# Paged attention on one core: the rotated heads turned by transposing DMAs instead of TensorE, with rows laid out position by batch

## The chip, the cores and the metric

The kernel runs on one core of a Trainium2 chip. The metric is the device time of one execution in microseconds; lower is better. Names of engines: TensorE (PE in the profile, PEld for its weight loads), VectorE (DVE), ScalarE (ACT), GpSimd (POOL), and SyncE (SP), which here only issues DMAs.

## The reference

`x` is 64 sequences of 32 positions by 512. Two residual layers follow each other; the second is where this change lies.

```python
x = x + L0(x)                                   # 512x512 product, weights quantized to a codebook plus LoRA
q = (x @ Wq.T).reshape(64, 32, 32, 128)         # 32 query heads
k = (x @ Wk.T).reshape(64, 32, 8, 128)          # 8 key heads
v = (x @ Wv.T).reshape(64, 32, 8, 128)
q, k = rope(rmsnorm(q, q_norm_w), pos), rope(rmsnorm(k, k_norm_w), pos)
k_all = concat([k_cache[block_table], k])       # 16 pages of 32 keys, then the 32 new ones
v_all = concat([v_cache[block_table], v])
probs = softmax(mask(q @ k_all.T / sqrt(128)))  # 4 query heads share a key head
x = x + (probs @ v_all).reshape(64, 32, 4096) @ Wo.T
```

## The kernel before

**Tiles and units.** 128 rows, 4 sequences of 32 positions, make a tile; there are 16 tiles, and each is done twice, once per half of the heads (4 key heads and 16 query heads), so the tile loop runs over 32 tiles. A tile has 16 units: 4 sequences ("batches") times 4 key heads. A unit's 128 query rows are 4 query heads of one key head by 32 positions of one batch. Most products are made of 16-bit high and low parts, three matmuls for one product.

**What a unit does.** `tile_block` writes every engine's program by hand, slot by slot (one slot per unit). On TensorE: scores of unit s against 512 cached keys (line 1204) and the 32 new ones (1207), the transposes of the probabilities of unit s-2 (1215), the output against the values of unit s-3 (1238, 1240), the turn of its new-key columns (1220). VectorE takes the row maxima (1448), normalises (1459) and makes low parts (1453, 1466); ScalarE does the exponentials (1353) and high parts. Scores of a unit wait until the maxima of the one before have been read from the single bank `Sp`.

**Heads of the next tile.** Between these, a tile also projects the next tile's heads, group by group: keys (group 0), queries (1, 3, 4, 5) and values (2). The table `TILE_PLAN` says in which slot each step stands: `proj` on TensorE, `squares` and `scale` on ScalarE, `root` and `add` on GpSimd, `rope` on VectorE. GpSimd's `add` ends the rotation: `qr` then holds 128 rows by 4 heads of 128 in 32 bits. Before the change `turn_rotated` transposes the four heads on TensorE into the bank `TRp` (line 1270, slots 5, 6, 10, 12, 14), and `rotated_high` on ScalarE (1397) and `rotated_low` on VectorE (1493) write high and low parts of it to `qT` or `kTn`, putting the columns batch by batch on the way. A tile's first scores wait for the last `tr_lo` of the tile before. `TRp` also serves 40 of the 56 weight pieces that are split during the loop (line 1281).

**SyncE's queue.** SyncE works through one list per batch: page numbers into registers, a wait for the maxima of the batch three back, that batch's mask (line 696), weight pieces where due (713, 716), the sixteen page loads of 64 KB for a buffer that has come free (688), and then, by the batch's place in the tile, stores and loads of new values (699, 703), the rope table (709), `xT` (706), the residual rows (1109, 1113). There are three page buffers, so pages are loaded two batches ahead. In the first 15 tiles or so the weight pieces add loads and stores to this list.

**Values.** GpSimd gathers the value rows of the next batch, four indirect DMAs per batch, in the slots set by `((0, 1), (2,), (3,), ())`.

**Before the loop.** A set-up block prepares caches and weights; at its end SyncE loads the first four tiles of `x` (line 447) and the first weights (449), and all engines meet at a barrier. `first_block` then makes the first layer's result for 16 tiles and the first tile's heads; its SyncE list loads `x` (776), stores the result (778) and its turned rows (781), loads weights (395) and the first pages.

## Time and profile before

| | us |
|---|---|
| runs, median of 3 (2249.0 to 2250.43) | 2250.25 |
| the profiled execution, whole time | 2244.9 |
| its span in the profile | 2243.0 |
| TensorE busy in the span | 2158.3 |
| first scores of the tile loop at | 306.30 |

The span runs from the first to the last instruction of the profiled execution; its whole time lies 1.9 us above it, and the median of the runs 5.35 us above that. Times in rows count from the span's start. A row of a timeline gives start, length, engine, line, operation and tiles; where TensorE's rows overlap, one matmul's end is still in the array while the next begins, so starts are compared with starts. A row of the SyncE queue is the time its issue took, not the transfer.

### The profile page before, as it was taken

How to read it: one execution, taken by the hardware profiler on the slowest of the kernel's cores; microseconds unless marked ns; L12 is line 12 of the kernel's file. 1: busy time of each engine (PE TensorE's matmuls, PEld its weight loads, DVE VectorE, ACT ScalarE, POOL GpSimd, SP SyncE). 2: the span in 40 equal slices, each digit the busy share in tenths (PEclk: the TensorE clock that was granted, in tenths of full speed). 3: DMA queues.
4: the chain of work that ended last, by engine and by line, in shares of the span. 5: the costliest groups of instructions: out<-in, count | busy, mean ns of one | idle time of the engine just before them, and what ended most of it. 6: DMA issues, size and time to landing. Idle time of an engine off the chain costs nothing.

```text
span 2243.0 us, 61281 instructions
## 1 busy us (share of the span) xinstructions
PE 2158.3 (96%) x18068; PEld 1411.6 (63%) x18068; DVE 1727.7 (77%) x3942; ACT 1465.5 (65%) x4967; POOL 1251.3 (56%) x2067
## 2 busy tenths in 40 slices
PE   5786989999999999999999999999999999999998
PEld 2343556666666666666666666666666666666665
DVE  6995668777777777777777777777777777777785
ACT  2542557676677776676676667667666666666664
POOL 3422126656666655665656666666656566665663
PEclk9997999999999999999999999999999999999999
DMA  3687658667667667667669667666566656666663
GB/s 103 221 279 248 222 167 238 195 193 207 200 194 207 197 191 216 203 198 211 198 191 300 179 189 238 185 177 175 175 188 181 181 173 186 183 178 177 184 178 104
DMA packets 478727, 438.06 MB, mean 195 GB/s; under 512 B 53037, under 2 KB 407676, under 8 KB 477886
## 3 DMA queue, kind: packets, MB, share of 16 engines
q1 hardware_dynamic: 433278, 295.70, 44.7%
q0 software_dynamic: 40960, 134.25, 19.6%
q10 hardware_dynamic: 4160, 4.19, 0.5%
q8 instruction: 149, 2.44, 0.4%
q14 instruction: 180, 1.47, 0.2%
HBM read 377.24 MB, written 56.70 MB: 193 GB/s over the span
## 4 chain that ended last, share of the span: by engine, by line
PE 84%; DVE 1%; issue 0%; ACT 0%; DVEq 0%; ACTq 0%
PE PR L1257 21%; PE Op L1238 15%; PE WOp L1296 15%; PE Sp L1204 15%; PE PTp L1215 11%; PE TRp L1270 3%; PE Sp L1207 1%; PE Op L1220 1%; PE Op L1240 1%; PE TRp L1281 1%; DVE masked L1448 0%; PE WOp L1281 0%; ACT masked L1353 0%; DVE WoT L1507 0%; DVE OT L1466 0%
## 5 line engine op out<-in xcount | busy, mean ns | idle before, releaser
L669 POOL DMA_INDIRECT pages<-values_split,rows x512 | 526.4, 1028 | 104.0 <-issue 78.5
L1347 ACT ACTIVATE pts<-PTp 128x512 f16<-128x512 f32 x512 | 305.7, 597 | 363.9 <-PE PTp L1215 363.8
L1257 PE MATMUL PR<-Wt,xT 128*128 128x512 f16 x2232 | 539.1, 380 | 0.0
L1238 PEld LDWEIGHTS Op<-pts,pages 128*128 128x128 f16 x6144 | 385.4, 98 | 121.1 <-DVE OT L1466 4.2
L1238 PE MATMUL Op<-pts,pages 128*128 128x128 f16 x6144 | 426.6, 219 | 2.4 <-DVE OT L1466 2.3
L1204 PE MATMUL Sp<-pages,qT 128*128 128x512 f16 x1536 | 416.2, 380 | 6.9 <-PEq L184 6.9
L1448 DVE CUSTOM_DVE_ANT_0 masked<-Sp,mask 128x544 f32<-128x544 f32 x512 | 370.0, 723 | 60.4 <-PE Sp L1207 54.3
L1453 DVE TENSOR_TENSOR pts<-PTp,pts 128x512 f16<-128x512 f32 x512 | 351.5, 686 | 75.1 <-ACT pts L1347 74.9
L1353 ACT ACTIVATE masked<-masked,small 128x544 f32<-128x544 f32 x512 | 379.0, 740 | 9.4 <-DVE small L1448 8.5
L1296 PE MATMUL WOp<-WoT,OT 128*128 128x512 f16 x1536 | 377.5, 379 | 0.0
L1466 DVE TENSOR_TENSOR OT<-Op,OT 128x128 f16<-128x128 f32 x512 | 148.2, 289 | 266.3 <-ACT p L1341 262.7
L1257 PEld LDWEIGHTS PR<-Wt,xT 128*128 128x128 f16 x2232 | 218.6, 98 | 187.6 <-issue 1.7
L1215 PE MATMUL PTp<-ident,masked 128*128 128x128 f32 x2048 | 325.1, 281 | 0.6 <-DVE pts L1453 0.6
L1558 POOL CAST n<-masked 128x64 f16<-128x64 f32 x512 | 120.8, 236 | 354.0 <-DVE masked L1459 217.6
L1459 DVE TENSOR_SCALAR masked<-masked,small 128x544 f32<-128x544 f32 x512 | 280.7, 548 | 18.2
L1362 ACT ACTIVATE OT<-Op 128x128 f16<-128x128 f32 x512 | 145.6, 284 | 205.3 <-PE Op L1220 197.0
L1296 PEld LDWEIGHTS WOp<-WoT,OT 128*128 128x128 f16 x1536 | 145.0, 98 | 116.4
L1215 PEld LDWEIGHTS PTp<-ident,masked 128*128 128x128 f32 x2048 | 214.2, 140 | 1.0 <-issue 0.8
L1204 PEld LDWEIGHTS Sp<-pages,qT 128*128 128x128 f16 x1536 | 142.3, 98 | 96.9 <-issue 8.2
L1551 POOL TENSOR_TENSOR qr<-qr,rs_ 128x512 f32<-128x512 f32 x155 | 196.8, 1270 | 0.0
L1207 PEld LDWEIGHTS Sp<-kTn,qT 128*128 128x128 f16 x1536 | 113.7, 97 | 121.4 <-issue 1.0
L1546 POOL TENSOR_TENSOR small<-small 128x4 f32<-128x4 f32 x155 | 181.9, 1174 | 12.9
(211 smaller groups left out, 3075.5 us busy)
## 6 DMA issues: line engine op xcount, KB each, us to landing
pages<-keys_transposed SPq DMA_DIRECT2D x2048, 64.0 KB
mask<-mask_rows SPq DMA_DIRECT2D x128, 128.0 KB
v<-new_values SPq DMA_DIRECT2D x96, 128.0 KB
weights_split<-wdst SPq DMA_DIRECT2D x40, 256.0 KB
keys_transposed<-pages SPq DMA_DIRECT2D x32, 256.0 KB, 3.4
values_split<-pages SPq DMA_DIRECT2D x16, 512.0 KB, 3.6
rope_s<-rope_table SPq DMA_DIRECT2D x32, 256.0 KB
pages<-values_split,rows POOLq DMA_INDIRECT x512
```

Source lines behind the costliest of these rows:

```text
L669: nc.gpsimd.indirect_dma_start(out=vS[:, n % 2, c, :, :].rearrange("p l n -> p (l n)"), out_offset=None, in_=v_d, in_offset=bass.IndirectO ...
L1204: nc.tensor.matmul(Sp[:, 512:1024].rearrange("p (a n) -> p a n", a=NPP), qT[:, tt, ql, q0:q0 + P], kT[n % KBUFS][:, :, h, kl, :], start=(k ...
L1215: m = nc.tensor.transpose(PTp[:, c * P:(c + 1) * P], masked[:, u % 3, S + c * P:S + (c + 1) * P], ident[:, :])
L1238: nc.tensor.matmul(o, vS[:, par, c, low, h * D:(h + 1) * D], pts[:, u % 2, part, c * P:(c + 1) * P], start=(k == 0), stop=False)
L1257: m = nc.tensor.matmul(bank(k), xT[:, c, xl, :], Wp[:, c, wl, GROUP_COL[k]:GROUP_COL[k] + HID], start=(i == 0), stop=(i == NPASS - 1))
L1296: m = nc.tensor.matmul(WOp[:, :], OT[:, 1 - tt, hq, ol, :], WoT[:, hq, wl, :], start=(hq == 0 and ol == 0 and wl == 0), stop=(hq == QHH - ...
L1347: nc.scalar.activation(pts[:, u % 2, 0, :], PTp[:, :], ACT.Copy).then_inc(G.pt_hi, 1)
L1353: nc.scalar.activation(masked[:, u % 3, :], masked[:, u % 3, :], ACT.Exp, bias=nmax[u % 2], scale=-1.0, accum_out=psum_row[u % 2]).then_in ...
L1448: V.tensor_tensor_reduce(out=masked[:, u % 3, :], in0=Sp[:, 512 - S:1024], in1=mask[:, par, :], scale=-SCALE, scalar=BIG, op0=ALU.add, op1 ...
L1453: V.tensor_tensor(pts[:, u % 2, 1, :], PTp[:, :], pts[:, u % 2, 0, :], ALU.subtract).then_inc(G.pt_lo, 1)
L1459: V.tensor_scalar(masked[:, u % 3, :], masked[:, u % 3, :], rinv[u % 2], None, ALU.mult).then_inc(G.norm_done, 1)
L1551: nc.gpsimd.tensor_tensor(qr[:, m_ % 2, :], qr[:, m_ % 2, :], rs_[:, :], ALU.add).then_inc(G.rope_done, 1)
```

## The change

The rotated heads are no longer transposed by TensorE. ScalarE and VectorE split `qr` into 16-bit high and low parts in a new tile `split` (two buffers), and SyncE issues one transposing DMA per group, 128 rows by 1024 columns, from `split` into `qT` or `kTn`. The first tile's heads, in `first_block`, are still turned by TensorE.

- `turn` in the plan now names places in SyncE's list: the batch in the tile, and which third of the page loads the DMA stands before (3: after them). `split` names the slots of the two halves of the split.
- [...] The scores read a batch's columns with a step of four elements (`b::BPT`), in `qT` and `kTn` alike.
- `qr` has one buffer instead of two; three small tables move into other memory.
- A tile's scores wait per key head, at the first batch, for the DMA of that head (`heads_turned`), instead of for all of `tr_lo`.
- Of the output product's early parts (`wo`), three matmuls move from slot 8 to slot 7 and three from slot 7 to slot 5.
- The fourth value gather of a batch is issued one slot earlier.

```diff
-    turn={5: 0, 6: 1, 10: 3, 12: 4, 14: 5}, turned={6: 0, 7: 1, 11: 3, 13: 4, 15: 5},
-    wo={4: (0, 1), 7: (1, 2), 8: (2, 3), 9: (3, 4), ...
+    split={5: 0, 7: 1, 10: 3, 12: 4, 14: 5}, turn={(0, 3): 0, (1, 1): 1, (2, 0): 3, (2, 3): 4, (3, 0): 5},
+    wo={4: (0, 1), 5: (1, 2), 7: (2, 3), 9: (3, 4), ...
...
                 for t in range(4):
-                    sp.dma_start(xin[:, t, :], x_d[t]).then_inc(G.x_first, 16)
+                    for b in range(BPT):
+                        sp.dma_start(xin[b::BPT, t, :], x_d[t, b * S:(b + 1) * S, :]).then_inc(G.x_first, 16)
...
         def load_table(sp, tile):
-            sp.dma_start(rope_s[:, :], rope_d[tile % TILES]).then_inc(G.table_loaded, 16)
+            for b in range(BPT):
+                sp.dma_start(rope_s[b::BPT, :], rope_d[tile % TILES, b * S:(b + 1) * S, :]).then_inc(G.table_loaded, 16)
...
                         if t < TPS + 4:
-                            sp.dma_start(out_d[t - 4], x1b[t % 2]).then_inc(x1_stored[t % 2], 16)
+                            for b in range(BPT):
+                                sp.dma_start(out_d[t - 4, b * S:(b + 1) * S, :], x1b[t % 2][b::BPT, :]).then_inc(x1_stored[t % 2], 16)
...
+                    def turn_heads(ti, k):
+                        m_ = norm_no(ti, k)
+                        sp.wait_ge(G.split_low, m_ + 1)
+                        sp.dma_start(turned_heads((ti + 1) % 2, k), split[:, m_ % 2, :, :].rearrange("p l n -> p (l n)"), transpose=True).then_inc(heads_turned[NORMED.index(k)], 16)
...
-                            for part in (range(0, 5), range(5, 10), range(10, NPP)):
+                            for third, part in enumerate((range(0, 5), range(5, 10), range(10, NPP))):
+                                if past >= 0 and ti in proj and (b, third) in plan["turn"]:
+                                    turn_heads(ti, plan["turn"][b, third])
                                 load_pages(sp, numbers, batch % KBUFS, part)
...
+                        if ti in proj and (b, 3) in plan["turn"]:
+                            turn_heads(ti, plan["turn"][b, 3])
...
-                        if u % UPT == 0 and u > 0:
-                            pe.wait_ge(G.tr_lo, len(NORMED) * (u // UPT))
-                        q0 = (h * BPT + b) * P
+                        if b == 0 and u >= UPT:
+                            if h == 0:
+                                pe.wait_ge(heads_turned[0], 16 * (u // UPT))
+                            pe.wait_ge(heads_turned[h + 1], 16 * (u // UPT))
+                        q = [qT[:, tt, h, part, b::BPT] for part in range(2)]
...
-                    def rotated_high(ti, tt, k):
-                        a.wait_ge(G.tr_done, norm_no(ti, k) + 1)
-                        src, dst = rotated(tt, k, 0)
-                        nc.scalar.activation(dst, src, ACT.Copy).then_inc(G.tr_hi, 1)
+                    def rotated_high(ti, k):
+                        m_ = norm_no(ti, k)
+                        a.wait_ge(G.rope_done, m_ + 1)
+                        if m_ >= 2:
+                            before, kb = divmod(m_ - 2, len(NORMED))
+                            a.wait_ge(heads_turned[kb], 16 * (before + 1))
+                        nc.scalar.activation(split[:, m_ % 2, 0, :], qr[:, :], ACT.Copy).then_inc(G.split_high, 1)
...
                         if m_ >= 1:
-                            v.wait_ge(G.rope_done, m_)
+                            v.wait_ge(G.split_low, m_)
...
-                    def rotated_low(ti, tt, k):
-                        v.wait_ge(G.tr_hi, norm_no(ti, k) + 1)
-                        src, dst = rotated(tt, k, 1)
-                        _, high = rotated(tt, k, 0)
-                        V.tensor_tensor(dst, src, high, ALU.subtract).then_inc(G.tr_lo, 1)
+                    def rotated_low(ti, k):
+                        m_ = norm_no(ti, k)
+                        v.wait_ge(G.split_high, m_ + 1)
+                        V.tensor_tensor(split[:, m_ % 2, 1, :], qr[:, :], split[:, m_ % 2, 0, :], ALU.subtract).then_inc(G.split_low, 1)
...
-                            for c in ((0, 1), (2,), (3,), ())[place]:
+                            for c in ((0, 1), (2, 3), (), ())[place]:
                                 gather(m + 1, c)
```

How the instructions move, at the places that matter. TensorE, from the end of slot 6 to the scores of slot 7 of a tile, before:

```order
L1238 MATMUL Op<-pts,pages 128x128 x12
L1240 MATMUL Op<-p,v 128x128
L1220 MATMUL Op<-ident,n 128x128
L1270 MATMUL TRp<-ident,qr 128x128 x4
L1204 MATMUL Sp<-pages,qT 128x512 x3
L1207 MATMUL Sp<-kTn,qT 128x32 x3
```

and with the change, at the same place:

```order
L1245 MATMUL Op<-pts,pages 128x128 x12
L1247 MATMUL Op<-p,v 128x128
L1227 MATMUL Op<-ident,n 128x128
L1211 MATMUL Sp<-pages,qT 128x512 x3
L1214 MATMUL Sp<-kTn,qT 128x32 x3
```

The four transposes into `TRp` are gone, at this place and at the four others of each tile.

VectorE, slots 5 and 6 of a tile with the change (line 1483 is the low part of the split, 1477 and 1478 are the rotation, 1487 the new values):

```order
L1441 ISA masked,small<-Sp,mask 128x544
L1441 ISA small 128x1
L1483 TENSOR_TENSOR split<-qr,split 128x512
L1446 TENSOR_TENSOR pts<-PTp,pts 128x512
L1477 TENSOR_TENSOR qr<-qn,rope_s 128x512
L1478 TENSOR_TENSOR rs_<-qn,rope_s 128x512
L1450 RECIPROCAL small<-small 128x1
L1452 TENSOR_SCALAR masked<-masked,small 128x544
L1459 TENSOR_TENSOR OT<-Op,OT 128x4x32
L1441 ISA masked,small<-Sp,mask 128x544
L1441 ISA small 128x1
L1487 SCALAR_TENSOR_TENSOR vn<-PR,vn 128x512
```

Before, the key heads' low part stood one slot later, just ahead of the new values; now it stands in the slot of the rotation of the first query group, after that slot's maxima.

SyncE, at the turn of a tile's last two batches, with the change (line 689 is a page load and the register step before it):

```order
L689 ISA
L689 DMA pages<-keys_transposed 128x256
L1113 DMA_TRANSPOSE qT<-split 128x8x128
L704 DMA v<-new_values 32x2048 x3
L684 DMA page_no<-page_numbers 1x128
L675 TENSOR_LOAD page_no
L697 DMA mask<-mask_rows 128x512
L1113 DMA_TRANSPOSE qT<-split 128x8x128
L689 ISA
L689 DMA pages<-keys_transposed 128x256
```

Before, the same list had no row between the last page load and the new values, nor between the mask and the next page loads.

## Rows read from the trace of the kernel before

**Rows 1.** The page's busy time of each engine, with its share of the span.
```profile
PE 2158.3 (96%) x18068; PEld 1411.6 (63%) x18068; DVE 1727.7 (77%) x3942; ACT 1465.5 (65%) x4967; POOL 1251.3 (56%) x2067
```

**Rows 2.** The page's chain that ended last: shares by engine and by line.
```profile
PE 84%; DVE 1%; issue 0%; ACT 0%; DVEq 0%; ACTq 0%
PE PR L1257 21%; PE Op L1238 15%; PE WOp L1296 15%; PE Sp L1204 15%; PE PTp L1215 11%; PE TRp L1270 3%; PE Sp L1207 1%; PE Op L1220 1%; PE Op L1240 1%; PE TRp L1281 1%; DVE masked L1448 0%; PE WOp L1281 0%; ACT masked L1353 0%; DVE WoT L1507 0%; DVE OT L1466 0%
```

**Rows 3.** Timeline of TensorE, 1240 to 1249 us: start, length, line, tiles.
```profile
1247.23 0.61 PE L1270 MATMUL TRp<-ident,qr 128*128 128x128 f32 x4
1247.67 0.81 PE L1204 MATMUL Sp<-pages,qT 128*128 128x512 f16 x3
1248.32 0.23 PE L1207 MATMUL Sp<-kTn,qT 128*128 128x32 f16 x3
1248.40 0.63 PE L1215 MATMUL PTp<-ident,masked 128*128 128x128 f32 x4
```

**Rows 4.** Timeline of the SyncE queue, one batch from 1235 us.
```profile
1235.05 0.32 SPq L696 DMA_DIRECT2D mask<-mask_rows  x1
1235.55 9.05 SPq L688 DMA_DIRECT2D pages<-keys_transposed  x16
```

**Rows 5.** SyncE's own waits: 366 to 1204, 1384 to 2102, 305 to 366 us.
```profile
SPq L696 <- DVE small L1448: 137.1, 53, 5.4
...
SPq L696 <- DVE small L1448: 158.3, 49, 4.6
...
SPq L713 <- PE WOp L1281: 5.1, 6, 1.8
```

**Rows 6.** Timeline of the SyncE queue: the load of xT in two early and two late tiles.
```profile
412.46 0.58 SPq L706 DMA_DIRECT2D xT<-x_transposed  x1
...
473.56 0.58 SPq L706 DMA_DIRECT2D xT<-x_transposed  x1
...
1803.25 0.43 SPq L706 DMA_DIRECT2D xT<-x_transposed  x1
...
1863.03 0.43 SPq L706 DMA_DIRECT2D xT<-x_transposed  x1
```

**Rows 7.** DMA view: a queue's share; issues by tile, size, us to landing.
```profile
q1 hardware_dynamic: 433278, 295.70, 44.7%
...
new_values<-vn SPq DMA_DIRECT2D x32, 256.0 KB, 2.3
...
pages<-in_L_cond_Wv SPq DMA_DIRECT2D x1, 1024.0 KB, 8.6
```

**Rows 8.** Timeline of the SyncE queue, 193 to 222 us.
```profile
194.07 1.79 SPq L447 DMA_DIRECT2D OT<-in_x  x4
195.91 0.43 SPq L449 DMA_DIRECT2D pages<-in_L_cond_Wk  x1
204.80 0.25 SPq L764 DMA_DIRECT2D page_no<-page_numbers  x1
...
205.52 0.50 SPq L709 DMA_DIRECT2D rope_s<-rope_table  x1
...
221.07 0.95 SPq L395 DMA_DIRECT2D pages<-in_L_cond_Wv  x1
```

**Rows 9.** Timeline of the first block: TensorE at 231 us, SyncE's queue at its end.
```profile
231.39 0.60 PE L849 MATMUL Op<-ident,pages 128*128 128x128 f32 x4
...
301.89 0.43 SPq L781 DMA_DIRECT2D x_transposed<-pts  x1
```

**Rows 10.** Groups by line and shape: weight loads of 16-bit and of 32-bit rows.
```profile
L1215 PEld LDWEIGHTS PTp<-ident,masked 128*128 128x128 f32 x2048 | 214.2, 140 | 1.0 <-issue 0.8
...
L1207 PEld LDWEIGHTS Sp<-kTn,qT 128*128 128x128 f16 x1536 | 113.7, 97 | 121.4 <-issue 1.0
```

**Rows 11.** Timeline of GpSimd and of ScalarE at unit 5 of a tile.
```profile
1238.96 1.27 POOL L1551 TENSOR_TENSOR qr<-qr,rs_ 128x512 f32<-128x512 f32 x1
...
1240.53 0.31 ACT L1341 ACTIVATE p<-Op 128x128 f16<-128x128 f32 x1
```

More of the change, by code:

```diff
@@ L129, in build @@
         qn = sb("qn", [P, 2, HID], F32)
[L130 removed]
+        qr = sb("qr", [P, HID], F32)
+        split = sb("split", [P, 2, 2, HID], F16)
         rs_ = sb("rs_", [P, HID], F32)
@@ L702, in load_new_values @@
             for place, part in enumerate((0, 1, 0)):
-                sp.dma_start(v5[place * S:(place + 1) * S, tile % 2, :, :], vn_d[tile % 2, part].rearrange("(b p) n -> p b n", b=BPT)).then_inc(v5_loaded[tile % 2], 16)
+                sp.dma_start(v5[place * S:(place + 1) * S, tile % 2, :, :], vn_d[tile % 2, part].rearrange("(p b) n -> p b n", b=BPT)).then_inc(v5_loaded[tile % 2], 16)
         def load_xT(sp, tile):
@@ L1079, in pieces_before @@
                 return sum(g < slot for g in piece_at)
-            def turns_before(slot):
-                return sum(UPT * t + sl < slot for t in proj for sl in plan["turn"])
             def unit(u):
@@ L1316, in _ @@
                             output(ti, tt, *plan["wo"][sl])
-                        if ti in proj and sl in plan["turn"]:
-                            turn_rotated(ti, plan["turn"][sl], sl)
                         if s in piece_at:
@@ L1410, in _ @@
                             new_probs(s - 3)
-                        if ti in proj and sl in plan["turned"]:
-                            rotated_high(ti, tt, plan["turned"][sl])
+                        if ti in proj and sl in plan["split"]:
+                            rotated_high(ti, plan["split"][sl])
                         if s - 1 in piece_at:
@@ L1516, in _ @@
                         if ti in proj:
-                            if sl in plan["turned"]:
-                                rotated_low(ti, tt, plan["turned"][sl])
+                            if sl in plan["split"]:
+                                rotated_low(ti, plan["split"][sl])
                             if sl == plan["values_low"]:
```

85 lines of the change are left out of this document (32 added, 53 removed).

## The prediction

> **What bounds the kernel now.** I read four views in turn. The busy shares first: TensorE is at 96%, the next engine, VectorE, at 77% [rows 1]. The chain that ended last says the same in another way: 84% of the span is TensorE, and the turning of rotated heads (line 1270) alone is 3% of the chain [rows 2]. Then TensorE's timeline inside a tile: the transposes of one head group begin at 1247.23 us and the next unit's scores at 1247.67 us, back to back with no idle time before either [rows 3]. So in the tile loop whatever leaves TensorE's stream shortens the kernel, as long as nobody else becomes late. Last, the SyncE queue, because that is where the work goes: for each batch of four units it issues sixteen page loads in about 9.05 us [rows 4], and the only wait it has left in the loop is for the maxima of the batch before (line 696). That wait is its slack: 137.1 us from 366 to 1204 us and 158.3 us from 1384 to 2102 us [rows 5]. From one load of xT to the next a tile takes 473.56 - 412.46 = 61.1 us in the first stretch and 59.8 us in the second [rows 6]; that is 13.7 and 12.0 tiles, so SyncE has 10.0 us to spare per early tile and 13.2 us per late one.
>
> **What leaves TensorE.** In the tile loop 155 turns (31 tiles, five each, four transposes a turn) are removed. A turn takes 1247.67 - 1247.23 = 0.44 us of the stream [rows 3]; 3% of 2243 us over 155 gives 0.43 us [rows 2]. Gain: 155 x 0.435 = 67.5 us, or 2.2 us a tile. The five turns of the first block stay.
>
> **What the other engines do instead.** ScalarE's and VectorE's halves of the split have the same size, 128 x 512, as the two evacuations they replace, now from SBUF and mostly a slot earlier. Do they find their input? For the key heads ScalarE gets to the place at 1240.53 + 0.31 = 1240.84 us, and GpSimd's addition has ended at 1238.96 + 1.27 = 1240.23 us [rows 11]: 0.6 us in hand, so no wait. The second order fence shows the piece on VectorE: rotation and split now fall in one slot. It is the same work per tile in a tile 2.2 us shorter; I allow 0.1 us a tile of lateness, 4 us in all. The earlier value gathers cost nothing: GpSimd issues the same four per batch, behind the new columns TensorE waits for.
>
> **What SyncE takes over.** Per tile, five transposing DMAs of 256 KB, and four rope loads instead of one. A single load takes the queue 0.43 to 0.50 us [rows 6, 8]; three smaller ones more make 1.25 us. A transposing DMA occurs nowhere in this trace. Below, it cannot cost less than a plain issue, 0.43 us [rows 8]; above, if the queue were held from issue until the data has landed, it would cost what a 256 KB store of similar size takes to land, 2.3 us [rows 7]. I take 1.4 us, the middle: neither row is near, since the queue has more to describe than for a copy but has no need to wait for the landing. With a price T per DMA a tile asks 1.25 + 5T of SyncE and gives back 2.2 us less time:
> early tiles gain the smaller of 2.2 and 10.0 - 1.25 - 5T; at T = 1.4 that is 1.75, a shortfall of 0.45 us x 14 tiles = 6 us. Late tiles gain the smaller of 2.2 and 13.2 - 1.25 - 5T = 4.95: all of it, in 16 tiles.
> The first tile has no such slack. There SyncE waits only 5.1 us, for weight pieces [rows 5], and 1.25 + 7 = 8.25 us are added: 3 us late. Bytes are no worry: 155 x 256 KB = 40.6 MB beside the 295.70 MB that took 44.7% of the DMA engines [rows 7], about 6 points more at the same rate.
> Behind a turn that waits for its split stand page loads and masks, two batches ahead of their use; the last turn of a tile is issued at the tile's end and needed by its fourth unit, three units of some 3.7 us later.
>
> **Before the loop.** The rows of inputs now go position by batch, so each 128-row load or store of x becomes four of 32 rows.
> The first x loads: 4 issues took 1.79 us, from 194.07 us on, the stage load behind them went at 195.91 us, and everything stood until 204.80 us [rows 8]. Twelve more issues at 1.79 / 4 = 0.45 us push that load back by 5.4 us, and nothing else runs there: 5 us, directly on the path.
> First block: the value weights were issued at 221.07 us [rows 8], take 8.6 us to land [rows 7], so about 229.7 us, and TensorE turns them at 231.39 us [rows 9]. Ahead of them come 1.25 us of rope loads and two steps with six more DMAs, less a gap: some 5.3 us later, so 235.0 us, 3.6 us too late.
> Its end: in the last four steps, up to the last store of the turned rows at 301.89 us [rows 9], SyncE is nearly always issuing, pages among the stores; four steps with three more stores are 5.2 us, and some 1.7 us of gaps absorb part: 3.5 us.
>
> **Strided reads.** The stationary rows of the scores now step over four elements (8 bytes), and no load of weights in this trace does that. Where 512 columns follow, a load is hidden behind them; the three loads for the new keys are not, since their matmuls come 0.08 / 3 = 0.027 us apart [rows 3]. Upper bound: a weight load of twice the bytes takes 140 ns and not 97 [rows 10], 43 ns x 1536 = 66 us, the whole gain. Lower bound: 0; a gain is excluded, since the same columns are read. I take 0: the strided load uses as many bytes as before, and the row of as many bytes is the one of 97 ns.
> The Trainium skill (SBUF — State Buffer, "Specifications (TRN2)") asks for two hits per 16-byte line for full bandwidth, and 8-byte steps give just two: by it the cost would be 0 as well, against the 66 us of the row. No run here shows it yet.
>
> **Sum.** -67.5 + 6 + 3 + 4 + 5 + 3.6 + 3.5 = -42.4 us. The profiled execution took 2244.9 us (span 2243.0 us), the median of the runs 2250.25 us, 5.35 us above; so 2202.5 us against the profile and **2208 us** against the median. Own range of this case: T = 1.2 with the smaller losses left out (up to -61 us) gives 2189; T = 1.7 (early tiles gain 0.25 us, the first loses 2.45) gives -3.5 - 35.2 + 2.45 + 16.1 = -20 us, 2230.
>
> **Rivals.**
> *SyncE becomes the bound (slower).* Place: the turns among the page loads; price: T. Early tiles lose once T passes 1.75, late ones keep the full 2.2 up to T = 1.95. The late tiles' -16 x 2.2, the early ones' 14 x (5T - 8.75), the first tile's 1.25 + 5T - 5.1 - 2.2 and the 16.1 us of the four other losses come to zero at T = 1.97: above that the kernel is slower. If the eight 128 x 128 blocks of a DMA are each issued like one small transfer (8 x 0.32 us [rows 4], T = 2.56), early tiles lose 4.05 us each, late ones 0.85, the first 6.75: 57 + 14 + 7 + 16 = 94 us, so 2344 us; at T = 2.3 it is 2303 us. For it: all is issued by one queue, in order, that is busy 84% of an early tile. Against: single issues of up to 1 MB took under 1 us [rows 8]. Chance 0.24.
> The Trainium skill speaks for it: VectorE: DVE Perf Modes, "The three transpose paths", gives 1309 ns for a 128 x 128 transpose by DMA against 390 ns on TensorE. If eight such followed one another with the queue held, T would be an estimated 10.5 us and the kernel beyond 3500 us; no run here shows it, and I give that extreme 0.03 of the 0.24.
> *Strided weight loads are slow.* The three short matmuls per unit wait; up to 66 us back: 2208 to 2274 us. For: nothing hides them. Against: they are 1536 short loads of the same bytes. Chance 0.09.
> *VectorE is late.* Split and rotation in one slot leave the probabilities' low halves late, TensorE waits in two or three slots per tile, 0.5 to 1 us a tile: 2223 to 2239 us. Chance 0.07.
> That the change does less than it says (turns still on TensorE) is excluded by the first order fence.
>
> **How the numbers follow.** Forecast 0.60 (2189 to 2230). Within 0.2% (4.5 us, about what a measurement can tell) lie T near 1.95 and a strided cost near its middle. Faster: 0.60 + 0.07 + 0.03 of strided reads = 0.70; same 0.06; slower 0.24. The range 2188 to 2290 holds the forecast, VectorE late, strided reads and the mild part of the SyncE rival; it leaves out T above 2.2, about 0.15.
>
> **What would show it.** Right: line 1270 gone, a late tile near 57.6 us, SyncE still waiting for maxima a few us per late tile, single DMA_TRANSPOSE rows near 1.4 us, the tile loop beginning some 12 us later. Wrong: SyncE without waits in the loop and TensorE idle before the scores of a tile's first units, released by a DMA; or the short score matmuls further apart than 0.027 us.

## The result, and the profile after

The changed kernel takes 2422.3 us (median of 4 runs, 2404.8 to 2431.4) against 2249.6 us (4 runs): a ratio of 1.076, 95% interval 1.070 to 1.083. It is 172.7 us **slower**; the forecast was 2208 us and the range ended at 2290 us. The profiled execution of the changed kernel took 2418.0 us, its span 2416.1 us.

The page of the changed kernel: busy time by engine, the load of SyncE's transfers (q1), and the chain that ended last.

```profile
PE 2169.8 (90%) x17448; PEld 1405.8 (58%) x17448; DVE 1725.4 (71%) x3942; ACT 1472.2 (61%) x4967; POOL 1263.9 (52%) x2067
...
q1 hardware_dynamic: 590814, 336.36, 55.0%
...
PE 45%; SPq 22%; issue 7%; DMA 6%; DVE 4%; ACT 2%; another core or an unknown queue 1%; DVEq 0%; ACTq 0%; POOL 0%
SPq L689 14%; PE WOp L1288 10%; PE PR L1264 9%; PE Op L1245 9%; PE Sp L1211 8%; PE PTp L1222 6%; DMA rope_s<-rope_table 4%; SPq L1113 3%; SPq L711 2%; DMA qT<-split 1%; PE Sp L1214 1%; SPq L704 1%; DVE qr L1477 1%; SPq L675 1%; DVE rs_ L1478 1%
```

Before, 84% of the chain was TensorE [rows 2]; now 45% is, and SyncE's queue with its transfers holds 28%. Among the links stands one that the prediction hardly spoke of: the load of the rope table. TensorE has 620 transposes less to do and yet a larger busy time than before [rows 1]; a lower granted clock will explain that.

The waits of VectorE, of TensorE and of the SyncE queue over the changed kernel's span (us in total, times, longest):

```profile
DVE qr L1477 <- DMA rope_s<-rope_table: 142.6, 30, 6.6
```
```profile
PE Op L1245 <- DVE OT L1459: 117.5, 49, 5.6
...
PE Sp L1211 <- DMA qT<-split: 12.9, 6, 5.0
```
```profile
SPq L697 <- DVE small L1441: 119.6, 55, 4.6
```

In every tile but the first the rotation of the key heads waits 142.6 / 30 = 4.75 us for the table; before, it waited once, 0.6 us. TensorE's long wait is for VectorE. SyncE still waits for maxima, 119.6 us in all, but, as will be seen, not in the batch where it would count. How one stall runs its course is in the chain of waits of the changed kernel, 1725 to 1739 us (start, length, what):

```profile
1725.26 4.15 DMA rope_s<-rope_table
1729.43 0.69 DVE qr L1477
1730.12 0.60 DVE rs_ L1478
...
1731.25 0.30 DVE OT L1459
1731.60 0.84 PE Op L1245 x12
...
1732.61 1.28 PE WOp L1288 x3
1733.89 1.28 PE Sp L1211 x3
...
1738.13 0.65 PE WOp L1288 x3
```

The four table loads of line 711 stand at the end of SyncE's list for a tile, behind the last turn and 16 page loads. The last one lands 4.15 us after the start of its issue. The rotation (lines 1477, 1478) runs then, and behind it, in VectorE's order, stands the low half of the output product (line 1459), for which TensorE's next value products wait.

Why the table is issued so late shows where the list of a tile's last batch is set beside the rotation that needs the table. The kernel before, SyncE's queue and VectorE:

```profile
1632.69 1.32 SPq L703 DMA_DIRECT2D v<-new_values  x3
...
1638.80 0.34 SPq L696 DMA_DIRECT2D mask<-mask_rows  x1
...
1648.01 0.42 SPq L709 DMA_DIRECT2D rope_s<-rope_table  x1
```
```profile
1654.15 0.68 DVE L1486 TENSOR_TENSOR qr<-qn,rope_s 128x512 f32<-128x512 f32 x1
```

and the changed kernel:

```profile
1708.30 1.27 SPq L1113 DMA_TRANSPOSE qT<-split  x1
1709.67 1.43 SPq L704 DMA_DIRECT2D v<-new_values  x3
1712.17 0.35 SPq L697 DMA_DIRECT2D mask<-mask_rows  x1
1712.63 1.25 SPq L1113 DMA_TRANSPOSE qT<-split  x1
1714.07 9.34 SPq L689 DMA_DIRECT2D pages<-keys_transposed  x16
1723.46 2.39 SPq L711 DMA_DIRECT2D rope_s<-rope_table  x4
```
```profile
1729.43 0.69 DVE L1477 TENSOR_TENSOR qr<-qn,rope_s 128x512 f32<-128x512 f32 x1 [4.42 <-DMA rope_s<-rope_table]
```

Before, the mask, which heads the list, starts 15.35 us ahead of the rotation, after a wait for maxima. In the changed kernel it starts 12.84 us ahead of the moment at which the rotation could have begun (1729.43 - 4.42 us): the list of the batch ahead, with two turns in it, ends only at 1711.10 us, and SyncE goes on without waiting for maxima. So the head of the list is 2.5 us late, and from the mask to the end of the table's issue the list takes 13.68 us in place of 9.63, 4.05 us longer. Over the 30 tiles the medians, taken from the two traces, are 2.7 us for the head and 4.4 us for the list. In 26 of the 30 tiles the changed kernel's last batch has no wait for maxima left at all; in the other four it is 1.1 us or less.

The timeline of TensorE gives the wait behind the late rotation:

```profile
1731.60 0.84 PE L1245 MATMUL Op<-pts,pages 128*128 128x128 f16 x12 [3.35 <-DVE OT L1459]
```

After these 3.35 us of idle time the twelve small matmuls still run at full speed (granted clock 1.00 up to 1732.3 us). The three matmuls of 512 columns behind them take 1.28 us, and some 5.5 us later three such take 0.65 us: between 1733 and 1735.5 us the granted clock is 0.50, which is the lower of TensorE's two levels, 1.2 GHz, and from 1736 us on it is 1.00 again, 2.4 GHz. Over the loop the stalls show in the windows of the changed kernel (length; busy time and instructions of PE, PEld, DVE, ACT, POOL; granted clock, DMA share, GB/s):

```profile
400.00:1290.00 890.00, 827.72 (x6977) 551.36 (x6975) 646.91 (x1568) 583.55 (x2028) 505.70 (x851) 0.97 0.84 207
1290.00:2190.00 900.00, 837.21 (x7023) 549.51 (x7021) 643.65 (x1575) 581.45 (x2031) 520.09 (x878) 0.97 0.76 197
```

In these two windows TensorE idles 125.1 us, and the granted clock is 0.97; in the kernel before it idled 1.3 us in the same two, the clock was 1.00 in both, and the DMA share was 0.70 and 0.63.

The loads of xT of the changed kernel (count, ns, first and last start) give a tile of (970.1 - 444.4) / 8 = 65.7 us early and (2268.3 - 1439.8) / 13 = 63.7 us late, in place of 61.1 and 59.8 us [rows 6]:

```profile
L707 SPq DMA_DIRECT2D xT<-x_transposed x9: 552/569/607, 444.4 to 970.1; - x9
```
```profile
L707 SPq DMA_DIRECT2D xT<-x_transposed x14: 431/432/1482, 1439.8 to 2268.3; - x14
```

The transposing DMAs of the changed kernel (ns min/median/max), and their landing:

```profile
L1113 SPq DMA_TRANSPOSE qT<-split x124: 1030/1256/5147, 365.2 to 2348.6; - x124
...
DMA to landing us min/median/max: 3.9/5.0/14.4
```

The start of the changed kernel on SyncE's queue answers to [rows 8]:

```profile
193.49 10.05 SPq L448 DMA_DIRECT2D OT<-in_x  x16
...
210.90 0.23 SPq L765 DMA_DIRECT2D page_no<-page_numbers  x1
...
211.64 2.41 SPq L711 DMA_DIRECT2D rope_s<-rope_table  x4
```

A DMA of 32 rows costs the queue 10.05 / 16 = 0.63 us, not the 0.45 us of a 128-row load. The barrier opens 6.1 us later (210.90 against 204.80 us), and the tile loop's first scores come at 329.1 us against 306.3 us, 22.8 us later. Not all of that is the change: three experiments below (e4, e12, e14) leave everything ahead of the tile loop as it was, and their first scores come at 311.6, 310.6 and 310.7 us. Against those the changed kernel is some 18 us later.

### The profile page after: what moved, and what is told of

Read it like the earlier page. It is cut to its first block, busy times and chain, and to the rows that moved or that the text cites. A ratio compares the mean times of both kernels' runs of the same rounds, so it can differ in the third digit from the quotient of the medians.

```text
span 2416.1 us, 60542 instructions
## 1 busy us (share of the span) xinstructions
PE 2169.8 (90%) x17448; PEld 1405.8 (58%) x17448; DVE 1725.4 (71%) x3942; ACT 1472.2 (61%) x4967; POOL 1263.9 (52%) x2067
## 3 DMA queue, kind: packets, MB, share of 16 engines
q1 hardware_dynamic: 590814, 336.36, 55.0%
q10 hardware_dynamic: 4160, 4.19, 0.5%
## 4 chain that ended last, share of the span: by engine, by line
PE 45%; SPq 22%; issue 7%; DMA 6%; DVE 4%; ACT 2%; another core or an unknown queue 1%; DVEq 0%; ACTq 0%; POOL 0%
SPq L689 14%; PE WOp L1288 10%; PE PR L1264 9%; PE Op L1245 9%; PE Sp L1211 8%; PE PTp L1222 6%; DMA rope_s<-rope_table 4%; SPq L1113 3%; SPq L711 2%; DMA qT<-split 1%; PE Sp L1214 1%; SPq L704 1%; DVE qr L1477 1%; SPq L675 1%; DVE rs_ L1478 1%
## 5 line engine op out<-in xcount | busy, mean ns | idle before, releaser
L1245 PE MATMUL Op<-pts,pages 128*128 128x128 f16 x6144 | 438.3, 222 | 120.6 <-DVE OT L1459 117.5
L1264 PE MATMUL PR<-Wt,xT 128*128 128x512 f16 x2232 | 546.0, 383 | 0.0
L1211 PE MATMUL Sp<-pages,qT 128*128 128x512 f16 x1536 | 429.7, 390 | 26.3 <-DMA qT<-split 12.9
L1441 DVE CUSTOM_DVE_ANT_0 masked<-Sp,mask 128x544 f32<-128x544 f32 x512 | 369.6, 722 | 92.5 <-PE Sp L1214 61.2
L1288 PE MATMUL WOp<-WoT,OT 128*128 128x512 f16 x1536 | 393.2, 391 | 0.0
L1548 POOL CAST n<-masked 128x64 f16<-128x64 f32 x512 | 138.5, 271 | 481.8 <-DVE masked L1452 386.8
L1222 PE MATMUL PTp<-ident,masked 128*128 128x128 f32 x2048 | 333.5, 287 | 6.3 <-DVE pts L1446 6.0
L1222 PEld LDWEIGHTS PTp<-ident,masked 128*128 128x128 f32 x2048 | 224.5, 145 | 7.3 <-issue 7.0
L1211 PEld LDWEIGHTS Sp<-pages,qT 128*128 128x128 f16 x1536 | 157.1, 115 | 118.6 <-issue 44.7
L1477 DVE TENSOR_TENSOR qr<-qn,rope_s 128x512 f32<-128x512 f32 x155 | 106.0, 684 | 142.6 <-DMA rope_s<-rope_table 142.6
L1214 PEld LDWEIGHTS Sp<-kTn,qT 128*128 128x128 f16 x1536 | 135.7, 117 | 112.2 <-issue 12.0
```

The costliest lines, as they stand in the source:

```text
L1211: nc.tensor.matmul(Sp[:, 512:1024].rearrange("p (a n) -> p a n", a=NPP), q[ql], kT[n % KBUFS][:, :, h, kl, :], start=(k == 0), stop=(k == 2))
L1222: m = nc.tensor.transpose(PTp[:, c * P:(c + 1) * P], masked[:, u % 3, S + c * P:S + (c + 1) * P], ident[:, :])
L1245: nc.tensor.matmul(o, vS[:, par, c, low, h * D:(h + 1) * D], pts[:, u % 2, part, c * P:(c + 1) * P], start=(k == 0), stop=False)
L1264: m = nc.tensor.matmul(bank(k), xT[:, c, xl, :], Wp[:, c, wl, GROUP_COL[k]:GROUP_COL[k] + HID], start=(i == 0), stop=(i == NPASS - 1))
L1288: m = nc.tensor.matmul(WOp[:, :], OT[:, 1 - tt, hq, ol, :], WoT[:, hq, wl, :], start=(hq == 0 and ol == 0 and wl == 0), stop=(hq == QHH - ...
L1441: V.tensor_tensor_reduce(out=masked[:, u % 3, :], in0=Sp[:, 512 - S:1024], in1=mask[:, par, :], scale=-SCALE, scalar=BIG, op0=ALU.add, op1 ...
```

## The experiments

Two theories were tested first. **A**: the table's landing, a deadline at the next tile's key rotation, makes the loop's loss, wherever SyncE's spare time lies. **B**: the sum of SyncE's list, five transposing DMAs in it, sets the tile's length. **C** stands beside them: strided weight loads cost a large part. All medians are set against the kernel before on the same chip, 2249.2 to 2249.9 us. In the diffs below, - is the kernel named in the sentence ahead, + the experiment, and ... stands for code left out.

### The table's load moved forward (e1)

The changed kernel, with the load put ahead of the wait for the scores, the last turn and the pages:

```diff
+                            if b == 3 and ti + 2 < NT:
+                                sp.wait_ge(G.rope_part, len(NORMED) * (ti + 1))
+                                load_table(sp, ti + 2)
                             sp.wait_ge(G.qk_done, KVH * (past + 1))
...
                         if b == 3:
-                            if ti + 2 < NT:
-                                sp.wait_ge(G.rope_part, len(NORMED) * (ti + 1))
-                                load_table(sp, ti + 2)
```

> The changed kernel with one thing moved: SyncE issues the four loads of the next tile's rope table in the last quarter of a tile ahead of the wait for the scores, the last turn and the 16 page loads, not behind them. Theory A (the table lands too late for the key heads' rotation at the next tile's head, and everything VectorE does behind it waits): the 142.6 us that the first L1477 of a tile waits for the table fall to under 10 us, the 117.5 us that the output products wait for VectorE to under 15, the granted clock of the loop comes back to 0.99 or more, and the time falls by 3.5 to 5 us per tile, to 2270 to 2315 us. Theory B (SyncE's list as a whole, with five transposing DMAs in it, sets the tile's length wherever the table stands in it): the wait moves from the table to another transfer (pages, turned heads), and the time stays above 2390 us.

Measured: 2310.7 us, ratio 1.026 (1.025 to 1.028); 111.6 us come back by moving one load, within A's band, 79 us below B's bound. TensorE's wait for output products falls to 7.5 us, and VectorE's wait for the table is gone. The granted clock of the second window is 0.99, of the first still 0.97, where A expected 0.99 for the loop. A new wait stands in the place of the table's; rows from the waits of e1's ScalarE, VectorE and TensorE:

```profile
ACT split L1390 <- DMA qT<-split: 72.5, 18, 10.2
```
```profile
DVE split L1483 <- ACT split L1390: 59.9, 15, 9.6
```
```profile
PE PTp L1222 <- DVE pts L1446: 49.7, 14, 8.8
```

The split has two buffers, and a buffer is free when the heads turned from it have landed. Where that is late, ScalarE's split waits, VectorE's low split behind it, and TensorE's next transposes behind that. The place differs, the course is the same: a late landing reaches TensorE through VectorE's order.

### The layout without the turns (e2), and the strided reads alone (e4)

e2 is the kernel before with x, table and output rows in DMAs of 32 rows (row = 4 x position + batch), strided scores and early gathers; TensorE still turns the heads. e4 is the kernel before with nothing but the step of four, in the new-key columns too; the columns that it reads are not those of one batch:

```diff
-                        q0 = (h * BPT + b) * P
+                        q = [qT[:, tt, part, h * HID + b:(h + 1) * HID:BPT] for part in range(2)]
...
```

> The kernel before with everything of the change but the turning of the heads: rows position by batch, so x, rope table and output rows in four DMAs of 32 rows, scores that read every fourth column, early value gathers; the heads are turned on TensorE as before. Theory A: the loop starts 20 us later as in the changed kernel, the scores cost some 0.02 us per unit more (10 us), and the table, which had 3.3 us in hand and now takes 1.9 us more of the queue, waits little: 2270 to 2295 us, more (up to 2340) if the table's 3.3 us don't hold. Theory B: the same first two terms, 2275 to 2290 us, and no wait for the table. Theory C (strided reads are a large part of the loop's loss): over 2330 us with TensorE's busy time up by more than 40 us.

> The kernel before where the scores read query and new-key columns at a step of four elements, in the places where the old layout stands, so the wrong columns are multiplied and the output is another; nothing else changes. All theories but C: the short score matmuls stand 0.033 us apart as in the changed kernel, not 0.027, and the weight loads take 115 to 120 ns, not 98: 0 to 12 us slower (2250 to 2262 us). Theory C: 40 to 66 us slower.

Measured: e2 2281.7 us (ratio 1.015, 1.013 to 1.016), e4 2258.8 us (1.0044, 1.0031 to 1.0058). So the strided reads cost 9.5 us, and C falls. e2's first scores come at 330.9 us, some 20 us later than in the kernels with an unchanged start; with 9.5 us that makes 29 us, and 32.4 us were measured. In e2 the key heads wait 0.6 us once for the table, though it comes in four loads there too: its issue ends 2.5 us later in the list (median), and the head of the list keeps its place. The layout explains 32 us of the 173; the other 140.6 us (2422.3 - 2281.7) lie with the turns and what came with them, the split, the single buffer of `qr` and the moved `wo` matmuls, which these two runs do not separate.

### Plain copies in place of transposing DMAs (e3), and both edits (e9)

e3 is the changed kernel with this edit, e9 has it on top of e1. The same bytes go to the same places, and the turning itself is left out:

```diff
-  ... split[:, m_ % 2, :, :].rearrange("p l n -> p (l n)"), transpose=True) ...
+  ... split[:, m_ % 2, :, :].rearrange("p l (r n) -> p (l r) n", r=REP)) ...
```

> The changed kernel with plain copies of the same bytes from the split heads to the same places in place of the transposing DMAs, so the heads are not transposed and the output is another. A plain copy's issue should hold SyncE's queue about 0.45 to 0.6 us in place of 1.26, so 3 to 4 us per tile come free on it. Theory A: the table is then issued some 2 us earlier (two or three of the five turns of a tile stand between its neighbours), so the wait for it halves at most: a fall of 1 to 2.5 us per tile, to 2340 to 2390 us. Theory B: the fall is the whole of what comes free, 3.5 us per tile or more, to 2310 us or less, and the wait for the table is gone.

> Both of e1 (table loaded early) and e3 (plain copies in place of transposing DMAs; the heads are not transposed, the output is another). If the late table and the transposing DMAs' time on SyncE's queue and the DMA engines are the two causes of all the loop's loss, nothing but the start (23 us) and the strided reads (9.5 us) is left over the kernel before, less whatever TensorE's 620 transposes left out now give: 2220 to 2285 us, the lower end if the gain of 2.2 us per tile comes through. If VectorE's or ScalarE's order (the split in one slot with the rotation) costs something of its own: over 2285 us.

Measured: e3 2295.5 us (1.0205, 1.0189 to 1.0220), e9 2246.1 us (0.9986, 0.9976 to 0.9997). e3 falls by 126.9 us, into B's band, but the table's wait is not gone, as B expected it to be: it falls from 142.6 to 58.3 us, 2.8 us a tile. The issue of a turn fell from 1.26 to 0.49 us, and three of a tile's five turns stand ahead of the table with no wait for maxima in between, two in the list of the third batch and one in that of the last. By the means of the two traces the head of the last list comes 1.5 us earlier and that list is 1.2 us shorter, 2.7 us together, while the time from the end of the table's issue to the rotation hardly moves (2.7 and 2.6 us). So the fall of the wait is time on the queue; the lighter DMA engines (share 0.74 and 0.68 in the windows, not 0.84 and 0.76) have little part in it. The edits overlap: 111.6 + 126.9 = 238.5 us apart, 176.3 us together. A and B are thus two sides of one thing, a landing that comes too late, by its place in the list and by the turns that the queue issues ahead of it.

### The rows turned elsewhere (e5), the table forward as well (e6)

e5 is the changed kernel with x, output rows and table in one DMA each again; the columns are sorted when x1 is evicted (ScalarE, and VectorE alike), and ScalarE stores the table sorted. e6 has the move of e1 as well:

```diff
-  ... x_turned(t)[:, :, 0, :], Sp[:, 0:512].rearrange("p (c n) -> p c n", c=IC), ...
+  ... x_turned(t)[:, :, 0, :].rearrange("p c (n b) -> p c n b", b=BPT), Sp[:, 0:512].rearrange("p (c b n) -> p c n b", c=IC, b=BPT), ...
...
-  a.dma_start(rope_d[ts_, :, ...] ..., rope_t[w][:, ts_, :, :] ...) ...
+  for b in range(BPT):
+      a.dma_start(rope_d[ts_, b::BPT, ...] ..., rope_t[w][b * S:(b + 1) * S, ts_, :, :] ...) ...
```

> The changed kernel with the same row order made elsewhere: x is loaded and the output rows stored in one DMA each, the eviction of the turned x1 writes its columns position by batch, ScalarE stores the rope table with permuted rows, and the tile's table comes in one load instead of four. The table's place behind the turns and pages stays. If 32-row DMAs at 0.6 us each make the late start (+23 us) and 1.9 us of the table's lateness: the first tile's scores come within 5 us of the kernel before (306 to 311 us), the wait of the rotation for the table falls from 4.6 us per tile to some 2.7, and the time is 2422 - 20 - 31 times 1.9 to 2.8 us = 2315 to 2345 us. If the table's place behind the turns alone makes it late (its own four issues do not matter): 2395 to 2405 us, the start's 20 us and no more.

> e5 and the table's load moved ahead of the last turn and pages as in e1. What e1 still lost against the kernel before was 61 us: 23 at the start, 9.5 for strided reads, and 29 in the loop, where the trace of e1 shows split buffers and scores waiting for the landing of turned heads. If those 29 us come from landings alone: 2310.7 - 20 and up to 10 us for a shorter list, 2280 to 2292 us. If they come from the length of SyncE's list: the 1.9 us per tile that the single table load frees come back as time, 2235 to 2255 us.

Measured: e5 2342.3 us (1.042, 1.038 to 1.046), e6 2278.9 us (1.011, 1.007 to 1.015). e5 is in the first band, though the steps are other than expected: the first scores come at 314.5 us and not by 311 us, since 16 table stores on ScalarE now delay the barrier (209.2 us; e11, which does without them, has 206.1), and the table's wait is 112.9 / 29 = 3.9 us and not 2.7. e6 is 1 us under its first band, far from the second. Of the 31.8 us that it lies under e1, 15.3 are the earlier start of the loop (314.9 against 330.2 us); the other 16.5 come from the loop, where early tiles fall from 63.9 to 62.7 us and late ones stay (58.6 and 58.5). So a shorter list gives something back in the early tiles, less than 1.9 us each, and some 12 to 16 us of loss are left in the loop (29.5 over the kernel before, less 4 to 8 for the start and 9.5 for strided reads). ScalarE still waits 49.5 us for turned heads.

### The turns on ScalarE's queue (e10), and its two leftovers mended (e11)

e10 is e6 with the turns taken out of SyncE's list and issued by ScalarE, in the slot after the split:

```diff
...
                         exps(s)
                         if ti in proj:
+                            if sl - 1 in plan["split"]:
+                                turn_heads(ti, plan["split"][sl - 1])
```

e11 is e10 with the positions themselves sorted early on, so the table comes out sorted, and the table's load first in the list of a tile's last batch:

```diff
+  for b in range(BPT):
+      g.dma_start(pos_turned[b::BPT, :], pos[b * S:(b + 1) * S, :]).then_inc(G.positions_turned, 16)
...
+  if b == 3 and ti + 2 < NT:
+      sp.wait_ge(G.rope_part, len(NORMED) * (ti + 1))
+      load_table(sp, ti + 2)
   sp.wait_ge(G.max_done, KVH * (past + 1))
```

> e6 with the five transposing DMAs of a tile issued by ScalarE on its own queue, in the slot after the split, behind the exponentials, so that they stand behind no page load. If turned heads land late because they queue behind pages on SyncE's list and rings: the landing falls from 5.0 us median and 14 us longest to under 4 and under 8, the waits of ScalarE's split and of the scores for turned heads go under 15 us together, and with 1.26 us more of ScalarE in 5 of 16 slots (it is busy 2.4 us of a slot's 3.6) the time is 2205 to 2250 us. If the landing is slow of itself, or ScalarE in front of the exponentials becomes the late one: over 2270 us.

> e10 with two things mended that its trace shows: the positions themselves are put in the new row order (four small DMAs early on), so the rope table is stored by 4 issues of ScalarE again in place of 16 and the first block's barrier, 5.0 us later in e10 than in the kernel before (209.82 against 204.80 us), comes back to within 1.5 us of it; and the table's load stands first in SyncE's list for a tile's last quarter, ahead of the mask, whose issue held the queue 9.1 us at the loading of the projection weights and made the one late table of e10 (10.3 us). If both are what e10 still loses: 2251 - 5 - 8 = 2234 to 2242 us, faster than the kernel before by 0.3 to 0.7%. If the DMA engines (94% busy in the early tiles of e10) or ScalarE's extra issues bind instead: no change from e10, 2245 to 2255 us.

Measured: e10 2251.1 us (1.0004, 0.9994 to 1.0015), e11 2249.8 us (1.0008, 0.9991 to 1.0025): both equal the kernel before, e10 1 us above the band expected, e11 as its second reading has it. The waits for turned heads are gone, but not because they land sooner. From the line of the turns in e10:

```profile
L1383 ACTq DMA_TRANSPOSE qT<-split x124: 1247/1249/3222, 348.2 to 2177.1; - x124
...
  PE Sp L1199: 2.1, 2
...
DMA to landing us min/median/max: 5.0/6.4/12.6
```

The median landing is 6.4 us, where under 4 us was expected; the turns are issued without a list ahead of them, and that is enough. e11 mends the barrier (206.1 us) and the table's one late landing, and gains nothing: early tiles take (977.2 - 426.6) / 9 = 61.2 us, late ones 58.8 us. Something else takes what 620 transposes gave.

### Plain copies on ScalarE's queue (e13)

e11 with the edit of e3; here too the turning is left out.

> e11 with plain copies of the same bytes in place of the transposing DMAs on ScalarE's queue (heads not transposed, another output). e11 has no wait for the table and none for turned heads, yet it only equals the kernel before although TensorE does 67 us less. If the load of the transposing DMAs on the DMA engines (their share is 93% in e11's early tiles, against 70% before) is what takes the gain: early tiles come from 61.2 to 59 us or less, late ones from 58.8 to 58 or less, and the time is 2200 to 2225 us. If the order of work on ScalarE and VectorE takes it: within 8 us of e11, 2242 to 2258 us.

Measured: 2205.4 us, ratio 0.980 (0.979 to 0.982), 44.4 us under e11, by a change in these DMAs alone. Early tiles take (951.5 - 418.5) / 9 = 59.2 us, late ones 58.4 us, both a little over the bounds expected. The windows and ScalarE's queue (packets, MB, share of 16 engines) of e11:

```profile
400.00:1290.00 890.00, 873.19 (x7523) 584.02 (x7522) 699.51 (x1694) 628.80 (x2177) 568.33 (x923) 1.00 0.93 227
1290.00:2190.00 900.00, 887.62 (x7683) 588.92 (x7680) 709.86 (x1725) 632.00 (x2215) 585.67 (x958) 1.00 0.85 209
```
```profile
q10 hardware_dynamic: 167840, 44.85, 13.3%
```

and of e13, with its busy times:

```profile
400.00:1290.00 890.00, 889.90 (x7758) 599.90 (x7756) 720.52 (x1742) 646.21 (x2240) 574.38 (x951) 1.00 0.77 233
1290.00:2190.00 900.00, 890.21 (x7778) 593.74 (x7777) 712.54 (x1740) 632.69 (x2196) 575.58 (x962) 1.00 0.69 207
```
```profile
PE 2104.3 (96%) x17448; PEld 1379.2 (63%) x17448; DVE 1729.8 (79%) x3942; ACT 1470.2 (67%) x4967; POOL 1287.7 (58%) x2071
...
q10 hardware_dynamic: 26480, 44.84, 5.6%
```

The bytes are the same. 4160 packets of this queue have nothing to do with the turns (that is its number in the changed kernel), so a transposing DMA makes (167840 - 4160) / 155 = 1056 packets and the plain copy 144. Together they take 0.133 x 2249.2 - 0.056 x 2202.6 = 176 us more of all 16 DMA engines, 1.1 us for each turn, and where the engines are at 93% that is time: in the first window e11's ScalarE waits for the stores of weight pieces to land, 15.4 us in 7 waits, and in e13's it waits 0.5 us once.

The issue on ScalarE falls too, from 1.25 to 0.47 us, and no run separates the two. The tiles bound it: ScalarE is as busy in e11's late window as in the early one (632.0 of 900 and 628.8 of 890 us) and issues five turns per tile in both, yet an early tile gains 2.0 us and a late one, at a DMA share of 0.85, 0.4 to 0.5. If the shorter issue counts alike in both, it is worth at most some 15 of the 44.4 us, an estimate from these rows.

### A late table in the kernel before (e12, e14)

Nothing of the change, only tiny copies ahead of the table's load, 12 in e12 and 4 in e14:

```diff
...
                                 sp.wait_ge(G.rope_part, len(NORMED) * (ti + 1))
+                                for i in range(12):
+                                    sp.dma_start(late_d[12 * ti + i], rope_d[0, 0, 0:NCB]).then_inc(G.late, 16)
                                 load_table(sp, ti + 2)
```

> The kernel before with 12 tiny copies between two DRAM tensors issued ahead of each rope table load, so that the table alone comes some 4 to 5 us later on SyncE's queue; they move 3 KB a tile. Theory A (a deadline at the next tile's key rotation, with about 3.3 us in hand): the first L1484-like rotation of each tile waits 1 to 2 us for the table, TensorE waits for VectorE's output products and then runs at the lower clock for a while: 30 tiles by 1 to 3 us, 2280 to 2340 us. If being late is absorbed by the slots of slack behind it (the theory falls): within 5 us of the kernel before, 2245 to 2255 us.

> As e12 with 4 tiny copies in place of 12, so the table of the kernel before comes 2.4 us later on the queue (0.59 us each, measured in e12). In e12 7.9 us of delay gave 7.0 us of waiting per tile, so 0.9 us was in hand, and each us of it cost 1.17 us of time: by that 1.5 us per tile wait and 31 times 1.7 us are added, 2290 to 2310 us. By the single tile read before the prediction 3.3 us were in hand: then 2.4 us is covered and nothing is added, 2245 to 2256 us.

Measured: e12 2495.2 us (1.110, 1.108 to 1.112), e14 2279.0 us (1.012, 1.010 to 1.014). e12 lies far above A's band: the copies cost more than expected, 0.59 us each at the median, 7.1 us of delay, and 7.89 us in the tile shown below; and less was in hand. VectorE's and TensorE's waits in e12:

```profile
DVE qr L1490 <- DMA rope_s<-rope_table: 209.9, 30, 8.9
```
```profile
PE Op L1242 <- DVE OT L1470: 181.7, 39, 7.8
```

and VectorE's in e14:

```profile
DVE qr L1490 <- DMA rope_s<-rope_table: 50.2, 29, 5.0
```

A table that is 7.0 us late per tile costs 245.3 / 30 = 8.2 us of time, at a DMA share that is lower than before (0.61 and 0.59) and with 313.4 us of SyncE's waits for maxima left in e12. One that is 1.7 us late costs 29.8 / 30 = 1.0 us, so e14 lies between the two readings of its expectation: of VectorE's 50.2 us of waiting only 26.1 reach TensorE, so part of the lateness is caught on the way; in e12 each us costs more than one, idle time and then the lower clock. What was in hand can be read from two late tiles: 6.1 us from the table's issue to the rotation before (1648.01 to 1654.15 us, shown above), 4.6 us where the rotation waits in e12:

```profile
1766.16 0.58 SPq L710 DMA_DIRECT2D rope_s<-rope_table  x1
```
```profile
1770.75 0.69 DVE L1490 TENSOR_TENSOR qr<-qn,rope_s 128x512 f32<-128x512 f32 x1 [6.82 <-DMA rope_s<-rope_table]
```

That makes some 1.5 us; the medians over 30 tiles of the two traces, 5.5 and 4.2 us, make 1.3. The deadline alone, in the kernel before, makes a loss larger than the change's.

## Why the prediction was wrong, point by point

- **The step that failed** stands in "What SyncE takes over": "three smaller ones more make 1.25 us". The table's load was priced as time on the queue and set against a tile's spare time. What counted was when it lands: SyncE's 10 to 13 us of slack per tile are four waits for maxima of some 3 us, one at the head of each batch's list, and the table is the last thing in a list. By the prediction's own formula, T = 1.26 leaves an early tile 10.0 - 1.25 - 6.3 = 2.45 us, more than the 2.2 it is to gain, so nothing should have been lost; but three of the five turns fall between the third batch's wait and the table, and use up the wait of the last batch. The table needs a row of its own in such a working: issued here, lands there, first user there. In the kernel before some 1.3 us were in hand. Against that the head of the last list came 2.7 us late and its list grew by 4.4 us: a turn (1.25 us and a short wait), four loads in place of one (1.9 us more), and somewhat slower page loads. These 7.1 us less the 1.3 in hand leave 5.8; the rotation waits 4.75, since the last of the four small loads lands some 1.1 us sooner after its issue than the one large load did in e12 (3.2 and 4.2 us, medians). The section on what is late behind a turn named page loads and masks, and not the table that stands right behind them.
- **T, the price of a transposing DMA on the queue**, was 1.26 us where 1.4 was taken; SyncE keeps 119.6 us of waits. The rival "SyncE becomes the bound" had the right sign and place, and a price from which it decides (T = 1.97) that was never reached, since it too pooled a tile's slack. In the sum the first tile's 3 us leave out 2.2 us that the rule for the early tiles would have added. The Trainium skill's 1309 ns for a 128 x 128 transpose by DMA (VectorE: DVE Perf Modes, "The three transpose paths") does not add up block by block here: eight such blocks held the queue 1.26 us and landed in 5.0 us.
- **"Bytes are no worry"** was the second failed step. The bytes were right (336.36 - 295.70 = 40.7 MB), but the 1056 packets of a turn were not priced: q1's share rose by 10 points, not 6. With the table's lateness cured, the transposing in e11 still cost 44 us over the plain copies of e13, all that the change had to give; at least some 30 of them go with the load on the DMA engines, by the estimate above, and the rest may be ScalarE's longer issue.
- **The gain of 67.5 us** is there for the most part: e13, which has neither lateness nor the packets, gains 43.8 us and still carries 9.5 us of strided reads, which makes 53 us. Its early tiles are 1.9 us shorter than before and its late ones 1.4; with 0.3 us a tile for the strided reads that is the 2.2 us forecast in early tiles and 1.7 in late ones. Where the rest went was not traced.
- **Before the loop** 12 us were forecast and some 18 to 23 us came, by the kernel that one compares with: 32-row DMAs at 0.63 us in place of 0.45, for the first loads and in every step of the first block.
- **Strided reads** were taken at 0 and cost 9.5 us: the weight load takes 114 ns and not 98 (medians of the short loads), and of these 16 ns some 6 show, as the short matmuls stand 0.033 us apart and not 0.027 (0.006 x 1536 = 9 us). The rule of the Trainium skill quoted there (SBUF — State Buffer, "Specifications (TRN2)"), two hits per 16-byte line, gave 0; the same row of that page adds that each cross to a new line pays a penalty, which the prediction left out. The measurement decides.
- **VectorE late** was a rival at 0.07 with 0.5 to 1 us per tile. VectorE did become the one TensorE waits for, not from its own work but from the load in front of its rotation.
- **The signs named**: the rows of 1.26 us and SyncE's waits came out as for a right prediction, the short score matmuls 0.033 us apart as for a wrong one, and a late tile took 63.7 us where 57.6 was the sign of a right one. "TensorE idle before the scores of a tile's first units, released by a DMA" was seen, but only 12.9 us of it; most of the idle time names VectorE as its releaser.

No version that turns the heads beat the kernel before: e10 and e11 equal it within 0.3%. Turning part of the tiles on TensorE, where the DMA engines are full, and a third split buffer were not tried.

## What to carry to other kernels

Slack of an in-order queue is not a sum over a tile: it lies where the queue waits, and work put between two waits uses up the second one only. For each transfer behind an inserted one, follow issue, landing and first user, above all for single-buffered tables at the end of a list. When work moves from an engine to DMA, count its packets and not its bytes, and read the DMA share of the stretch in which it will run. A wait of one small load can cost more than its length (245.3 us for 209.9 us of waiting in e12), since TensorE falls to the lower clock behind it.

## What was not expected of the hardware

- Behind a stall of 3.35 us TensorE ran its first small matmuls at 2.4 GHz still and then some 3 us at 1.2 GHz (granted clock 0.50 from 1733 to 1735.5 us). Over the run that is visible in the busy time: the same 17448 instructions are 2169.8 us busy in the changed kernel (granted clock 0.957) and 2104.3 us in e13 (0.988).
- A transposing DMA makes 1056 packets where a plain copy of the same 256 KB makes 144; it takes 1.25 us to issue on either queue, and lands in 5.0 us (SyncE) or 6.4 us (ScalarE, e10, with a DMA share of 0.94 and 0.86 in the two windows against 0.84 and 0.76).
- Small is not cheap on a queue: a 32-row DMA took 0.6 us and a copy of 256 bytes 0.59 us, a page load of 64 KB 0.33 us.
- A stationary operand (the one that a weight load puts into TensorE) read at a step of 8 bytes loads in 114 ns and not 98.
